# P transposed by VectorE's 32x32 blocks and a way through DRAM, in all attention steps of a gated cross-attention block

## The chip, the cores and the metric

One core of a Trainium2 chip. The metric is the device time of one execution in microseconds (us); the profile gives one execution's span from the first to the last instruction.

## The reference

Eight batches of 128 tokens with 512 features attend to 128 context tokens each, with 32 heads of width 128; a gated feed-forward with low-rank experts follows.

```python
def xattn(hidden, kv, mask, bias, ln_w, w_q, w_k, w_v, w_out):
    x = rmsnorm(hidden, ln_w)
    h_q, h_k, h_v = heads(x @ w_q.T), heads(kv @ w_k.T), heads(kv @ w_v.T)
    score = einsum('bqhd,bkhd->bhqk', h_q, h_k) + position_bias[None]
    score = where(m, score, -inf)
    score = where(m, softmax(score, axis=-1), 0.0)
    attn = einsum('bhqk,bkhd->bqhd', score, h_v).reshape(b, lq, H * DH)
    return hidden + attn @ w_out.T

x = x + tanh(g_xattn[0]) * xattn(layernorm(x), ctx, mask, ...)
x = x + tanh(g_ffn[0]) * ffn(layernorm(x), ...)   # base + LoRA experts, top 2 of 8
```

## The kernel before

The host only lays arrays out. Four stages follow each other. First the V product for all heads, spilled to DRAM (`v_spill`). Then the attention stage: 16 pairs of heads with four steps each, 64 steps (`s = 4 * p + j`), one step for one head and four of the eight batches (`HT`). Then the output product over 56 units, and the feed-forward. The large products are written as seven half-size products (M1 to M7) in place of eight, and each fp32 operand is split into a high and a low fp32r part, so that a product is three passes (`three_passes`, line 328).

The order of the work is written out by hand, one program for each engine, joined by semaphores. In the attention stage TensorE's step `s` does the scores of step `s + 1`, two or one products of the next pair's Q and K (`SLOT_PRODUCTS`), the four transposes of P (`transposes`), more products, and the attention of step `s`. In the last pair the output units 0 to 7 take the place of the products.

Each product needs its weights split. ScalarE makes the high part (`wq_hi`, line 797), VectorE the low part (`lo`, line 1014) and the sums of weights (`wq_sum`, lines 1133 to 1147), both directly after the product whose place in a ring of four units (`WRING`) is free; ScalarE copies and VectorE adds the products out of PSUM (`product_done`).

The softmax of a step: VectorE adds scores and masked bias (`scores`, line 1180, from bank 1 to the SBUF tile `pr`) and takes the negative maximum (1182); ScalarE takes the exponential of four 128x128 blocks with their sums (`softmax_exp`, 860); VectorE inverts the sums (1188), multiplies them with `allowed` (1190) and multiplies P (1193, `probabilities`, the last work of VectorE's step); TensorE transposes P into bank 2; ScalarE copies it to `pt_sb` (916); TensorE multiplies it with V (`attention`, 1531); ScalarE copies the result (`copy_attention`, 898). GpSimd prepares the masked bias (`mask_step`) and forms sums of attention results (`t_sum`, at the steps of `T_SUMS`).

One queue, SP's, issues every DMA, in program order: stores of attention results and their sums (`store_at`, `store_sums`), loads of V (`load_v`), of weights (`load_wq`) and of bias, pieces of the output weight (`load_piece`, `store_piece`), and late in the stage the first loads of the output stage (`EARLY_LOADS`, whose splits are at `EARLY_SPLITS`). A wait there holds up all that is queued behind it.

Of the kernel before, what the change touches and what calls it, by code (L numbers as in the profile page):

```python
# [61 lines left out]
T_SUMS = ((1, 0, 3), (1, 1, 5), (2, 1, 6), (2, 0, 7), (3, 1, 7), (4, 0, 8), (3, 0, 9), (4, 1, 10))  # L62
# [23 lines left out]
def flamingo_block(nc, x, ctx_t, mask, gates, bias, ln_w, w_qk, w_v, w_o, w_base, w_lora, w_up, b_base, out):  # L86
    v_dram = nc.dram_tensor("v_spill", (PAIRS, 2, 2, P, HALF, P), F32, kind="Internal").ap()
    t_dram = nc.dram_tensor("t_spill", (NP, DUOS, P, 2, W), F32, kind="Internal").ap()
    s_dram = nc.dram_tensor("s_spill", (NP, DUOS, P, 2, 2 * P), F32, kind="Internal").ap()
    stack = ExitStack()  # L90
    with stack:
# [46 lines left out]
        with second:  # L138
# [7 lines left out]
            pt_sb = sb("pt_sb", [P, W], on=second)  # L146
            pr = sb("pr", [P, 2, W], on=second)
# [61 lines left out]
        ps_s, ps_t, ps_at = bank[1], bank[2], bank[3]  # L209
# [30 lines left out]
        t_ps, pt_ok, a_ps, at_ok = sem("t_ps"), sem("pt_ok"), sem("a_ps"), sem("at_ok")  # L240
# [66 lines left out]
        def cols(k):  # L307
            return slice(P * k, P * k + P)

# [55 lines left out]
        def _(sp):  # L365
# [23 lines left out]
            def store_v(g, m):  # L389
                r, n = QUARTER[m]  # L390
                for t in range(HALF):
# [6 lines left out]
                    sp.dma_start(dst, stage[:, t, :, :]).then_inc(v_stored[t], 16)  # L398

# [122 lines left out]
            for p in range(PAIRS):  # L522
                if p + 2 < PAIRS:
                    sp.wait_ge(wq_lo_ok, NP * (p + 1))
                    load_wq(p + 2)
                for j in range(4):
                    s = 4 * p + j
                    store_at(s)
                    if s + VRING < STEPS:
                        sp.wait_ge(a_ps, s + 1)  # L530
                        load_v(s + VRING)
                    store_sums(s)
                    if s % 2 == 0 and s + 2 < STEPS:
                        store_piece(s // 2)
                    elif s % 2 and s + 1 < STEPS:
                        load_piece((s + 1) // 2)
                    if j == 2 and p + 2 < PAIRS:
                        sp.wait_ge(bm_ok, 4 * p + 4)
                        load_bias(p + 2)
                    for n in EARLY_LOADS.get((p, j), ()):  # L540
                        load_o(n)

            store_piece(STEPS // 2 - 1)
            for n in range(FIRST_LOAD, UNITS):
                load_o(n)
                if n < FIRST_LOAD + 3:
# [30 lines left out]
        def _(pool):  # L577
# [129 lines left out]
            for s in range(STEPS, STEPS + 3):  # L707
                t_sums(s)
# [18 lines left out]
        def _(act):  # L727
# [129 lines left out]
            def softmax_exp(s):  # L857
                act.wait_ge(nmax_ok, s + 1)
                for k in range(HALF):
                    last = act.activation(pr[:, s % 2, cols(k)], pr[:, s % 2, cols(k)], ACT.Exp, bias=nmax[:, k:k + 1],  # L860
                                          accum_out=sums[:, k:k + 1])
                last.then_inc(exp_ok, 1)

# [60 lines left out]
            copy_attention(STEPS - 1)  # L924
# [53 lines left out]
            for n in range(FIRST_SPLIT, 50):  # L978
                o_hi(n)
# [32 lines left out]
        def _(ve):  # L1012
# [162 lines left out]
            def scores(s):  # L1175
                ve.wait_ge(s_ps, s + 1)
                ve.wait_ge(bm_ok, s + 1)
                if s >= 2:
                    ve.wait_ge(t_ps, s - 1)
                ve.tensor_tensor(pr[:, s % 2, :], ps_s[:, :], bm[:, :, :].rearrange("p b n -> p (b n)"), ALU.add).then_inc(scored, 1)  # L1180
                ve.wait_ge(scored, s + 1)
                ve.tensor_reduce(nmax[:, :], pr[:, s % 2, :].rearrange("p (b k) -> p b k", b=HALF), AX.X, ALU.max,  # L1182
                                 negate=True).then_inc(nmax_ok, 1)

            def probabilities(s):
                n = HT[s % 4][1]
                ve.wait_ge(exp_ok, s + 1)
                ve.reciprocal(rinv[:, :], sums[:, :]).then_inc(inv_ok, 1)
# [557 lines left out]
```

## Time and profile before

| | |
|---|---|
| median of 3 runs | 820.06 us (819.56 to 820.52) |
| profiled execution | span 817.2 us; its time outside the span is not shown |
| busy | TensorE 99%, VectorE 78%, ScalarE 61%, GpSimd 36% |
| granted TensorE clock | 1.000 |
| DMA | 168.52 MB, 63.0% of 16 engines' span |

Busy shares are means over all stages; the attention stage is read by windows and by the instructions in order of time. The chain is the work that ended last, followed back from the end.

### The profile page before, as it was taken

To read this page: it belongs to the slowest core of one execution; us is meant where nothing else is said; L and a number is where in the kernel's file an instruction comes from. 1 tells how busy PE (TensorE), PEld (TensorE's weight loads), DVE (VectorE), ACT (ScalarE), POOL (GpSimd) and SP (SyncE) were. 2 spreads that over 40 slices of the span, in tenths; PEclk is the share of its full clock that TensorE was granted. 3 is DMA by queue.
4 is the path that set the end of the run, shared out by engine and by line. 5 is a ranking of instruction groups with operands and counts; after the bars stand their busy time and mean duration, and the time that the engine had idled before them with its cause. 6 is when DMAs were issued, how large, how long until landed. Compare 5 with 4: busy or idle time off the path is not lost.

```text
span 817.2 us, 13043 instructions
## 1 busy us (share of the span) xinstructions
PE 810.3 (99%) x4286; PEld 689.3 (84%) x4286; DVE 638.7 (78%) x997; ACT 497.1 (61%) x1164; POOL 294.5 (36%) x309
## 2 busy tenths in 40 slices
PE   9999999999999999999999999999999999999998
PEld 7787887888888888888888888888888788888886
DVE  6976476557887898688888888977887976789875
ACT  4646655447666666766666666667677677666311
POOL 1113230002456365455555563564733600003230
PEclk9999999999999999999999999999999999999999
DMA  9565455688545665565575466655598999997011
GB/s 324 157 194 169 118 165 168 218 247 257 168 146 190 189 199 161 193 212 149 180 220 173 147 192 187 189 172 193 173 308 308 367 387 386 328 325 263 20 46 59
DMA packets 132594, 168.52 MB, mean 206 GB/s; under 512 B 9392, under 2 KB 84016, under 8 KB 132272
## 3 DMA queue, kind: packets, MB, share of 16 engines
q1 hardware_dynamic: 132528, 167.70, 63.0%
q8 instruction: 35, 0.57, 0.3%
q14 instruction: 31, 0.25, 0.1%
HBM read 111.04 MB, written 62.91 MB: 213 GB/s over the span
## 4 chain that ended last, share of the span: by engine, by line
PE 90%; DVE 7%; issue 1%; ACT 1%; POOL 1%; DMA 1%; DVEq 0%; SPq 0%; POOLq 0%
PE bank L328 71%; PE bank L1514 7%; PE bank L1531 7%; PE bank L1522 3%; DVE t_hl L1014 1%; DVE s_hl L1014 1%; DVE stats L1018 1%; DVE wv L1014 1%; DMA raw_v<-in_w_v 1%; PE bank L1620 0%; PE bank L1457 0%; DVE stage L1075 0%; DVE acc L1250 0%; POOL xs L598 0%; DVE cb L1014 0%
## 5 line engine op out<-in xcount | busy, mean ns | idle before, releaser
L328 PE MATMUL bank<-cb,wq 128*128 128x512 f32 x672 | 177.2, 399 | 0.0
L328 PE MATMUL bank<-xb,wq 128*128 128x512 f32 x672 | 177.2, 399 | 0.0
L328 PE MATMUL bank<-t_hl,s_hl 128*128 128x512 f32 x672 | 158.0, 393 | 0.1
L328 PE MATMUL bank<-wv,cb 128*128 128x512 f32 x672 | 154.7, 391 | 1.5 <-DVE wv L1014 1.1
L328 PEld LDWEIGHTS bank<-wv,cb 128*128 128x128 f32 x672 | 125.6, 188 | 29.6 <-DVE wv L1014 3.0
L328 PEld LDWEIGHTS bank<-t_hl,s_hl 128*128 128x128 f32 x672 | 124.6, 188 | 26.2 <-DVE s_hl L1014 0.6
L654 POOL TENSOR_TENSOR bm<-bias_sb,mneg 128x512 f32<-128x512 f32 x64 | 74.6, 1166 | 197.4 <-DVE pr L1180 161.5
L328 PEld LDWEIGHTS bank<-cb,wq 128*128 128x128 f32 x672 | 121.9, 189 | 22.8
L328 PEld LDWEIGHTS bank<-xb,wq 128*128 128x128 f32 x672 | 121.8, 189 | 22.7
L860 ACT ACTIVATE pr<-pr,nmax 128x128 f32<-128x128 f32 x256 | 99.3, 394 | 7.2 <-DVE nmax L1182 7.2
L1014 DVE TENSOR_TENSOR t_hl<-t_raw,t_hl 128x1024 fp32r<-128x1024 f32 x56 | 72.1, 1287 | 21.0 <-ACT t_hl L871 20.8
L871 ACT ACTIVATE t_hl<-t_raw 128x1024 fp32r<-128x1024 f32 x56 | 59.3, 1059 | 41.8 <-PE bank L328 31.9
L1014 DVE TENSOR_TENSOR wq<-sq,wq 128x512 fp32r<-128x512 f32 x64 | 67.2, 1060 | 10.0 <-ACT wq L797 10.0
L1014 DVE TENSOR_TENSOR wq<-raw,wq 128x512 fp32r<-128x512 f32 x48 | 38.9, 812 | 42.9 <-ACT wq L797 42.7
L1531 PEld LDWEIGHTS bank<-pt_sb,v_sb 128*128 128x128 f32 x512 | 66.9, 191 | 5.0
L1514 PE MATMUL bank<-k_sb,q_sb 128*128 128x128 f32 x512 | 67.6, 275 | 0.0
L1531 PE MATMUL bank<-pt_sb,v_sb 128*128 128x128 f32 x512 | 67.3, 274 | 0.0
L1514 PEld LDWEIGHTS bank<-k_sb,q_sb 128*128 128x128 f32 x512 | 62.5, 192 | 0.2
L797 ACT ACTIVATE wq<-sq 128x512 fp32r<-128x512 f32 x64 | 40.1, 628 | 26.0 <-PE bank L328 26.0
L1180 DVE TENSOR_TENSOR pr<-bank,bm 128x512 f32<-128x512 f32 x64 | 43.9, 686 | 9.2 <-PE bank L1514 9.2
L860 ACT ACTIVATION_READ_ACCUMULATOR pr<-pr,nmax 128x1 f32 x256 | 49.5, 193 | 0.0
L1193 DVE TENSOR_TENSOR pr<-pr,rinv 128x512 f32<-128x512 f32 x64 | 46.1, 720 | 2.2
(158 smaller groups left out, 1169.9 us busy)
## 6 DMA issues: line engine op xcount, KB each, us to landing
t_raw<-t_spill SPq DMA_DIRECT2D x56, 512.0 KB, 5.5
v_spill<-stage SPq DMA_DIRECT2D x64, 256.0 KB, 3.1
raw<-in_w_qk SPq DMA_DIRECT2D x32, 512.0 KB, 5.8
v_sb<-v_spill SPq DMA_DIRECT2D x64, 256.0 KB, 3.1
s_raw<-s_spill SPq DMA_DIRECT2D x56, 256.0 KB, 5.6
t_spill<-x_at SPq DMA_DIRECT2D x48, 256.0 KB, 3.3
s_piece<-in_w_o SPq DMA_DIRECT2D x64, 128.0 KB, 3.5
s_spill<-s_piece SPq DMA_DIRECT2D x32, 256.0 KB, 3.6
```

The costliest lines, as they stand in the source:

```text
L328: mm = pe.matmul(dst, a, b, start=first and n == 0, stop=last and n == total - 1, skip_group_check=True)
L654: pool.tensor_tensor(bm[:, :, :], head_bias, mneg[:, HALF * n:HALF * n + HALF, :], ALU.add).then_inc(bm_ok, 1)
L797: act.activation(wq[:, u % WRING, 0, :, :], wq_source(p, m), ACT.Copy).then_inc(wq_hi_ok, 1)
L860: last = act.activation(pr[:, s % 2, cols(k)], pr[:, s % 2, cols(k)], ACT.Exp, bias=nmax[:, k:k + 1], accum_out=sums[:, k:k + 1])
L871: act.activation(t_hl[n % ORING][:, 0, :, :], t_raw[n % ORING][:, :, :], ACT.Copy).then_inc(o_hi_ok, 1)
L1014: return ve.tensor_tensor(dst, src, hi.bitcast(F32), ALU.subtract)
L1018: ve.bn_stats(stats[:, t, :], source(t)).then_inc(bn_sem, 1)
L1180: ve.tensor_tensor(pr[:, s % 2, :], ps_s[:, :], bm[:, :, :].rearrange("p b n -> p (b n)"), ALU.add).then_inc(scored, 1)
L1193: ve.tensor_tensor(own, own, rinv[:, :].unsqueeze(2).to_broadcast([P, HALF, P]), ALU.mult).then_inc(pr_ok, 1)
L1514: last = pe.matmul(ps_s[:, cols(k)], q_sb[:, j, cols(k)], k_sb[:, j, cols(k)], start=True, stop=True)
L1522: last = pe.transpose(ps_t[:, cols(k)], pr[:, s % 2, cols(k)], ident[:, :])
L1531: last = pe.matmul(ps_at[:, cols(k)], v_sb[:, s % VRING, k, :], pt_sb[:, cols(k)], start=True, stop=True)
```

## The change

TensorE's transposes and ScalarE's copy of P are gone. The scores of a step are written to one of two PSUM banks (1 and 2) and stay there: VectorE adds the bias in place, ScalarE takes the exponential in place, and ScalarE, not VectorE, multiplies P by the inverse sums (`scale_rows`). VectorE then turns P by 32x32 blocks from PSUM into the SBUF tile `turned` (`turn`, the first work of its step). SP stores the four groups of 32 partitions with four DMAs to DRAM (`p_spill`), so that the blocks come to their places, and loads the whole with one DMA into one of two tiles `pt`. Attention reads its four batches from it in runs of 32 columns, and stands one step later; the copy, the store of its result, the load of V and GpSimd's sums move with it. The attention of the last step stands behind output unit 9.

```diff
-T_SUMS = ((1, 0, 3), (1, 1, 5), (2, 1, 6), (2, 0, 7), (3, 1, 7), (4, 0, 8), (3, 0, 9), (4, 1, 10))
+T_SUMS = ((1, 0, 4), (1, 1, 6), (2, 1, 7), (2, 0, 8), (3, 1, 8), (4, 0, 9), (3, 0, 10), (4, 1, 11))
+LATE_SUMS = 4
+LAST_ATTENTION = 9
+QUADS = 4
+QUAD = P // QUADS
+TURN_EVERY = 1
...
+    p_dram = nc.dram_tensor("p_spill", (2, P, QUADS, P), F32, kind="Internal").ap()
...
-        ps_s, ps_t, ps_at = bank[1], bank[2], bank[3]
+        pr, ps_at = [bank[1], bank[2]], bank[3]
...
+        def pt_batch(s, k):
+            return pt[:, s % 2, :].rearrange("p (i k q) -> p k i q", i=QUADS, k=HALF)[:, k, :, :]
...
+            def store_turned(s):
+                sp.wait_ge(turned_ok, turns(s) + 1)
+                for i in range(QUADS):
+                    sp.dma_start(p_dram[turns(s) % 2, :, i, :].rearrange("(j c) n -> c j n", j=QUADS),
+                                 turned[QUAD * i:QUAD * i + QUAD, :].rearrange("c (j n) -> c j n", j=QUADS)).then_inc(turned_stored, 16)
+            def load_pt(s):
+                sp.wait_ge(turned_stored, 16 * QUADS * (turns(s) + 1))
+                if s >= 2:
+                    sp.wait_ge(a_ps, s - 1)
+                sp.dma_start(pt[:, s % 2, :], p_dram[turns(s) % 2, :, :, :].rearrange("p i n -> p (i n)")).then_inc(pt_in[s % 2], 16)
...
             for p in range(PAIRS):
                 for j in range(4):
                     s = 4 * p + j
+                    if by_quads(s):
+                        store_turned(s)
+                    if j == 0 and p + 2 < PAIRS:
+                        sp.wait_ge(wq_lo_ok, NP * (p + 1))
+                        load_wq(p + 2)
+                    if s % 2 and s + 1 < STEPS:
                         store_piece(s // 2)
                     if j == 2 and p + 2 < PAIRS:
                         sp.wait_ge(bm_ok, 4 * p + 4)
                         load_bias(p + 2)
+                    if by_quads(s):
+                        load_pt(s)
+                    store_sums(s)
+                    if s:
+                        store_at(s - 1)
+                        if s - 1 + VRING < STEPS:
+                            sp.wait_ge(a_ps, s)
+                            load_v(s - 1 + VRING)
+                    if s % 2 and s + 1 < STEPS:
+                        load_piece((s + 1) // 2)
...
+            def scale_rows(s):
+                act.wait_ge(inv_ok, 2 * s + 2)
+                into = pr[s % 2]
+                for k in range(HALF):
+                    last = act.activation(into[:, cols(k)], pr[s % 2][:, cols(k)], ACT.Copy, scale=rinv[:, k:k + 1])
+                last.then_inc(pr_ok, 1)
...
-                    copy_attention(s - 1)
+                    scale_rows(s)
+                    copy_attention(s - 2)
                     for n in range(done, done + before):
                         product_done(n)
-                    act.wait_ge(t_ps, s + 1)
-                    if s:
-                        act.wait_ge(a_ps, s)
-                    act.activation(pt_sb[:, :], ps_t[:, :], ACT.Copy).then_inc(pt_ok, 1)
                     if s + 1 < STEPS:
                         softmax_exp(s + 1)
...
-                ve.wait_ge(inv_ok, 2 * s + 2)
-                own = pr[:, s % 2, :].rearrange("p (b k) -> p b k", b=HALF)
-                ve.tensor_tensor(own, own, rinv[:, :].unsqueeze(2).to_broadcast([P, HALF, P]), ALU.mult).then_inc(pr_ok, 1)
+            def turn(s):
+                ve.wait_ge(pr_ok, s + 1)
+                if turns(s):
+                    ve.wait_ge(turned_stored, 16 * QUADS * turns(s))
+                ve.transpose(turned[:, :].rearrange("p (j k n) -> p j k n", j=QUADS, k=HALF),
+                             pr[s % 2][:, :].rearrange("p (k j n) -> p j k n", k=HALF, j=QUADS)).then_inc(turned_ok, 1)
...
+                    if by_quads(s):
+                        turn(s)
                     if s + 1 < STEPS:
                         scores(s + 1)
...
             def attention(s):
-                pe.wait_ge(pt_ok, s + 1)
+                pe.wait_ge(pt_in[s % 2], 16 * (s // 2 + 1))
...
-                        for n in range(done, done + before):
-                            product(n)
-                    else:
-                        output(2 * j)
-                    transposes(s)
-                    if p + 1 < PAIRS:
-                        for n in range(done + before, done + before + after):
+                        for n in range(done, done + before + after):
                             product(n)
                         done += before + after
                     else:
+                        output(2 * j)
                         output(2 * j + 1)
-                    attention(s)
+                    if s:
+                        attention(s - 1)
```

## Rows read from the trace of the kernel before

**Rows 1.** The page: busy time of each engine, and the chain by engine.
```profile
PE 810.3 (99%) x4286; PEld 689.3 (84%) x4286; DVE 638.7 (78%) x997; ACT 497.1 (61%) x1164; POOL 294.5 (36%) x309
...
PE 90%; DVE 7%; issue 1%; ACT 1%; POOL 1%; DMA 1%; DVEq 0%; SPq 0%; POOLq 0%
```

**Rows 2.** Window: busy us of PE, PEld, DVE, ACT, POOL; clock, DMA share, GB/s.
```profile
300.00:600.00 300.00, 300.00 (x1746) 260.91 (x1745) 248.06 (x393) 199.05 (x583) 158.91 (x169) 1.00 0.59 185
```

**Rows 3.** The chain in order of time: start us, us, what, 380 to 420 us.
```profile
386.48 0.44 PE bank L1522 x4
...
389.68 0.89 PE bank L1531 x8
...
400.55 0.44 PE bank L1522 x4
```

**Rows 4.** Groups of VectorE: busy us, mean ns of one, idle before.
```profile
L1014 DVE TENSOR_TENSOR t_hl<-t_raw,t_hl 128x1024 fp32r<-128x1024 f32 x56 | 72.1, 1287 | 21.0 <-ACT t_hl L871 20.8
L1014 DVE TENSOR_TENSOR wq<-sq,wq 128x512 fp32r<-128x512 f32 x64 | 67.2, 1060 | 10.0 <-ACT wq L797 10.0
...
L1180 DVE TENSOR_TENSOR pr<-bank,bm 128x512 f32<-128x512 f32 x64 | 43.9, 686 | 9.2 <-PE bank L1514 9.2
...
L1143 DVE TENSOR_TENSOR sq<-raw 128x512 f32<-128x512 f32 x16 | 18.4, 1150 | 0.0
...
L1133 DVE TENSOR_TENSOR sq<-raw 128x512 f32<-128x512 f32 x16 | 10.9, 684 | 0.2 <-DMA raw<-in_w_qk 0.2
...
L1258 DVE TENSOR_SCALAR xn<-acc,mv,scales 128x512 f32<-128x512 f32 x8 | 4.2, 542 | 0.6 <-POOL scales L714 0.6
```

**Rows 5.** Groups of ScalarE.
```profile
L916 ACT ACTIVATE pt_sb<-bank 128x512 f32<-128x512 f32 x64 | 37.9, 592 | 15.4 <-PE bank L1522 15.4
L873 ACT ACTIVATE s_hl<-s_raw 128x512 fp32r<-128x512 f32 x56 | 34.5, 616 | 0.0
...
L782 ACT ACTIVATE tok<-bank,lnw 128x512 f32<-128x512 f32 x8 | 4.8, 688 | 1.3 <-PE bank L1457 1.3
...
L946 ACT ACTIVATE h_sum<-bank 128x136 f32<-128x136 f32 x8 | 1.8, 281 | 6.1 <-PE bank L1622 6.1
```

**Rows 6.** ScalarE in order of time, in two stretches: start us, us, instruction.
```profile
393.85 0.40 ACT L860 ACTIVATE pr<-pr,nmax 128x128 f32<-128x128 f32 x1
...
395.39 0.58 ACT L846 ACTIVATE tmp<-bank 128x512 f32<-128x512 f32 x1
395.87 0.62 ACT L797 ACTIVATE wq<-raw 128x512 fp32r<-128x512 f32 x1
...
797.52 0.46 ACT L946 ACTIVATE h_sum<-bank 128x136 f32<-128x136 f32 x2 [1.20 <-PE bank L1622]
```

**Rows 7.** VectorE in order of time, 396 to 399 us.
```profile
396.52 0.69 DVE L1014 TENSOR_TENSOR wq<-raw,wq 128x512 fp32r<-128x512 f32 x1 [1.28 <-ACT wq L797]
...
397.73 0.17 DVE L1188 RECIPROCAL rinv<-sums 128x4 f32<-128x4 f32 x1
397.94 0.16 DVE L1190 TENSOR_TENSOR rinv<-rinv,allowed 128x4 f32<-128x4 f32 x1
398.13 0.69 DVE L1193 TENSOR_TENSOR pr<-pr,rinv 128x512 f32<-128x512 f32 x1
398.74 0.68 DVE L1180 TENSOR_TENSOR pr<-bank,bm 128x512 f32<-128x512 f32 x1
```

**Rows 8.** Who waited for whom: us in total, times, longest us.
```profile
DVE wq L1014 <- ACT wq L797: 52.7, 52, 2.5
```

**Rows 9.** DMA issues: KB each, median us from issue to landing.
```profile
v_spill<-stage SPq DMA_DIRECT2D x64, 256.0 KB, 3.1
raw<-in_w_qk SPq DMA_DIRECT2D x32, 512.0 KB, 5.8
v_sb<-v_spill SPq DMA_DIRECT2D x64, 256.0 KB, 3.1
```

**Rows 10.** SP's issues in order of time.
```profile
405.68 0.43 SPq L410 DMA_DIRECT2D v_sb<-v_spill  x1
```

More of the change, by code:

```diff
@@ L145, in flamingo_block @@
             bm = sb("bm", [P, HALF, P], on=second)
-            pt_sb = sb("pt_sb", [P, W], on=second)
-            pr = sb("pr", [P, 2, W], on=second)
+            turned = sb("turned", [P, W], on=second)
+            pt = sb("pt", [P, 2, W], on=second)
             x_at = sb("x_at", [P, 2, W], on=second)
@@ L308, in cols, with by_quads, turns @@
             return slice(P * k, P * k + P)
+        def by_quads(s):
+            return s % TURN_EVERY == TURN_EVERY - 1
+        def turns(s):
+            return s // TURN_EVERY
+        def pt_batch(s, k):
+            return pt[:, s % 2, :].rearrange("p (i k q) -> p k i q", i=QUADS, k=HALF)[:, k, :, :]
         def v_evac(g, m, t):
@@ L545, in _ @@
                 load_o(n)
-                if n < FIRST_LOAD + 3:
+                if n < FIRST_LOAD + LATE_SUMS:
+                    if n == FIRST_LOAD + LATE_SUMS - 2:
+                        store_at(STEPS - 1)
                     store_sums(STEPS + n - FIRST_LOAD)
@@ L706, in _ @@
             s_sums(STEPS // 2 - 1)
-            for s in range(STEPS, STEPS + 3):
+            for s in range(STEPS, STEPS + LATE_SUMS):
                 t_sums(s)
@@ L859, in softmax_exp @@
                 for k in range(HALF):
-                    last = act.activation(pr[:, s % 2, cols(k)], pr[:, s % 2, cols(k)], ACT.Exp, bias=nmax[:, k:k + 1],
+                    last = act.activation(pr[s % 2][:, cols(k)], pr[s % 2][:, cols(k)], ACT.Exp, bias=nmax[:, k:k + 1],
                                           accum_out=sums[:, k:k + 1])
                 last.then_inc(exp_ok, 1)
+            def scale_rows(s):
[4 more added lines that the diff above has]
+                last.then_inc(pr_ok, 1)
             def o_hi(n):
@@ L1177, in scores @@
                 ve.wait_ge(bm_ok, s + 1)
-                if s >= 2:
-                    ve.wait_ge(t_ps, s - 1)
-                ve.tensor_tensor(pr[:, s % 2, :], ps_s[:, :], bm[:, :, :].rearrange("p b n -> p (b n)"), ALU.add).then_inc(scored, 1)
+                own = pr[s % 2][:, :]
+                ve.tensor_tensor(own, own, bm[:, :, :].rearrange("p b n -> p (b n)"), ALU.add).then_inc(scored, 1)
                 ve.wait_ge(scored, s + 1)
-                ve.tensor_reduce(nmax[:, :], pr[:, s % 2, :].rearrange("p (b k) -> p b k", b=HALF), AX.X, ALU.max,
+                ve.tensor_reduce(nmax[:, :], own.rearrange("p (b k) -> p b k", b=HALF), AX.X, ALU.max,
                                  negate=True).then_inc(nmax_ok, 1)
@@ L1510, in scores @@
                     pe.wait_ge(ed_ok, 6 * p + 2 * j + 2)
-                if s:
-                    pe.wait_ge(scored, s)
+                if s >= 2:
+                    pe.wait_ge(turned_ok, s - 1)
                 for k in range(HALF):
-                    last = pe.matmul(ps_s[:, cols(k)], q_sb[:, j, cols(k)], k_sb[:, j, cols(k)], start=True, stop=True)
+                    last = pe.matmul(pr[s % 2][:, cols(k)], q_sb[:, j, cols(k)], k_sb[:, j, cols(k)], start=True, stop=True)
                 last.then_inc(s_ps, 1)
-            def transposes(s):
-                if s:
-                    pe.wait_ge(pt_ok, s)
-                pe.wait_ge(pr_ok, s + 1)
-                for k in range(HALF):
-                    last = pe.transpose(ps_t[:, cols(k)], pr[:, s % 2, cols(k)], ident[:, :])
-                last.then_inc(t_ps, 1)
             def attention(s):
-                pe.wait_ge(pt_ok, s + 1)
+                pe.wait_ge(pt_in[s % 2], 16 * (s // 2 + 1))
                 pe.wait_ge(v_in[s % VRING], 16 * (s // VRING) + 16)
@@ L1530, in attention @@
                 for k in range(HALF):
-                    last = pe.matmul(ps_at[:, cols(k)], v_sb[:, s % VRING, k, :], pt_sb[:, cols(k)], start=True, stop=True)
+                    last = pe.matmul(ps_at[:, cols(k)].rearrange("p (i q) -> p i q", i=QUADS), v_sb[:, s % VRING, k, :],
+                                     pt_batch(s, k), start=True, stop=True)
                 last.then_inc(a_ps, 1)
@@ L1644, in _ @@
                 output(n)
+                if n == LAST_ATTENTION:
+                    attention(STEPS - 1)
             out_transposes(0)
```

24 lines of the change are left out of this document (9 added, 15 removed).

## The prediction

> **What bounds the kernel now.** The page first. TensorE's matmuls cover 99% of the span and carry 90% of the chain that ended last [rows 1]: whatever another engine does is free as long as TensorE never waits for it. Then one stretch inside the attention stage, 300 to 600 us [rows 2]. TensorE is busy for the whole 300 us at a granted clock of 1.00 (the level of 2.4 GHz), VectorE for 248.06 and ScalarE for 199.05. Third the chain in order of time [rows 3]: four transposes of P take 0.44 us of it, eight attention matmuls 0.89. The transposes of every second step start 14.07 us apart (386.48 and 400.55), so a step is 7.03 us on average, a pair of heads (four steps, one round of `SLOT_PRODUCTS`) 28.14. In a mean step VectorE works 248.06/300 x 7.03 = 5.82 us and idles 1.22; ScalarE works 4.67. These 1.22 us of VectorE are all the room there is before it sets the pace.
>
> The second thing to read is why VectorE idles at all. Of its waits, 52.7 us in 52 cases are for ScalarE's high part of a weight unit [rows 8]; one is seen at 396.52, 0.03 us behind ScalarE's instruction of 395.87 [rows 6, 7], which had stood behind four exponentials and a copy. So part of that idle time is ScalarE's order and stays when the pace changes.
>
> **TensorE's side.** Removed: `transposes`, 64 x 0.44 = 28.2 us, all on the chain [rows 3]. Scores and attention keep their number of matmuls. P is now read in four runs of 32 columns; no row shows such a read. Below, it costs nothing; above, I bound it by a quarter more of the 0.89 us, 0.2 per step, within what TensorE gains. I take nothing: all operands are fp32 in rows as before. If TensorE remained the bound, the span would be 817.2 - 28.2 = 789.0.
>
> **ScalarE's side.** Removed: the copy of P out of PSUM, 0.592 us [rows 5], in a row of copies 0.48. Added: `scale_rows`, four 128x128 activations with a scale read per partition. The nearest row is a 128x136 copy from PSUM, 0.280; a per-partition scale lengthens a 128x512 copy from 0.592 to 0.688, so 0.10 more; one is 0.37 [rows 5]. Two of the 128x136 copies take 0.46 together, so they overlap by 0.10 [rows 6], and four scalings take 3 x 0.27 + 0.37 = 1.18. Bounds: 0.28 + 3 x 0.18 = 0.82 if the scale costs nothing, 4 x 0.40 = 1.60 if each takes an exponential's full record [rows 6]. The exponentials now read PSUM; copies do so in 0.592 where they take 0.616 from SBUF [rows 5], so four go from 4 x 0.385 = 1.54 (393.85 to 395.39 [rows 6]) to 1.44. ScalarE ends near 5.2 us a step and is not the bound by its sum.
>
> The Trainium skill (ScalarE: Activation LUTs, Rules for kernel authors) advises to leave multiplications to VectorE, which speaks against moving this one. Its prices (What ACT_TABLE_LOAD costs: 186 ns plus 0.833 per element, 93 for a pointer operand, 93 of overlap) would make an estimate of 1.27 for the four instead of the 1.18 of the rows, and the sum below 5 us larger. The rows decide.
>
> **VectorE's side.** Removed: the multiplication of P, 0.69, with 0.61 until the next one starts (398.13 to 398.74 [rows 7]). Added: the turn of 128x512 from PSUM, which no row shows. Below, 0.542, the quickest 128x512 instruction; above, 1.287, the instruction over twice the columns [rows 4]. I take 0.69, that of the PSUM operations of this size (L1180), because it reads PSUM at this width; occupancy 0.61. The score addition writes PSUM instead of SBUF; I leave it and the maximum at 0.69. In work VectorE neither gains nor loses.
>
> The Trainium skill (VectorE: DVE Perf Modes, The three transpose paths) gives 311 ns for 128x128 in bf16; four of these, an estimate, would be 1.24 and the sum 60 x 0.55 = 33 us larger; no row here shows a transpose on VectorE.
>
> What counts is the new wait. `probabilities(s)` is the last thing in VectorE's step and `turn(s)` the first of the next, with nothing between. Before, the multiplication followed the inverse by 0.03. Now VectorE hands the inverse over (0.04), stands still for the four scalings (1.18), takes over (0.04) and turns. It loses 1.23 us in every step, queued behind the wait are score addition, maximum, all weight splits and sums, and TensorE waits for those. Occupied time is 5.82 + 1.23 = 7.05 in the mean, already more than 7.03, before any other wait.
>
> **A pair laid out.** From the inverse on: head 0.04 + 1.18 + 0.04 + 0.61 + 0.72 (addition) + 0.60 (maximum) = 3.19 until VectorE is free, and the exponentials start at 3.32. Tail (reciprocal and small product): 0.40, from 397.73 to 398.10 [rows 7] and a little. Weight splits take 1.06 from sums in the mean [rows 4], from raw weights 0.69 undisturbed (396.52 [rows 7]); additions occupy 0.60; the four weight sums, one a step, take 0.684 (the first) to 1.150 (the third) in the mean [rows 4]. The steps of a pair, by `j`:
> Step 0: 3.19 + sum 1.07 + splits 0.90 and 0.80 + addition 0.60 + 0.40 = 6.96. Step 3: 3.19 + two additions 1.20 + split 0.87 + sum 1.10 + 0.40 = 6.76. In both, the splits needed are ready on ScalarE.
> Step 1 hangs on ScalarE: 3.32 + 1.44 (exponentials) + 0.48 (copy of M6) + 0.62 (high part) + 0.03 + split 0.70 + sum 0.62 + 0.40 = 7.61. Step 2 likewise: 3.32 + 1.44 + 0.62 + 0.03 + 0.70 + 0.85 + 0.40 = 7.36.
> Together 28.69. These layouts hold 22.2 us of VectorE's work (four heads without the wait 7.7, four tails 1.6, and 3.4, 2.9, 3.4, 3.2 in the steps, with what runs hidden behind ScalarE in steps 1 and 2), where the rows have 248.06/300 x 28.14 = 23.27; the 1.07 missing are splits and sums that last longer than I set them. Half lies in steps 0 and 3, and a little more behind the waits of 1 and 2: I add 0.65. A pair is 29.34, 7.33 a step, 1.20 more than before.
>
> **DMA and SP.** Per step four stores of 64 KB and a load of 256 KB come on SP's queue, 33.6 MB in all. The landing rows are 3.1 us for the 256 KB store in 512-byte rows and for the V load [rows 9]; issuing takes 0.43 [rows 10]. From the inverse of step s: attention s-2 is copied at 1.73, behind the scalings; SP issues its store, the V load and in odd steps two pieces (to 2.6 or 3.7); four stores (the last begins at 3.9 or 4.9); landed at 7.0 or 8.0; load landed at 10.1 or 11.1. The weight loads, piece store and bias load that are queued behind the four stores fill that wait. `attention(s)` stands at the end of TensorE's next step, takes 0.89 and must be through at 2 x 7.33 - 0.5 = 14.1, since scores and the first product of the step behind it are wanted early; 11.1 + 0.89 = 12.0, so at least 2 us are left, which hide the way. The next turn waits for the stores until 8.0 and comes at 7.33 + 1.26 = 8.6. GpSimd's sums move by one step with their sources and cost nothing, hidden in its 53% of use [rows 2]. With 0.5 MB more per step the DMA share goes from 0.59 [rows 2] to some 0.8.
>
> **The sum.** Fifteen pairs x 1.20 = +18.0. In the last pair the splits of the output stage stand between inverse and turn on VectorE and hide the scalings; there TensorE stays the bound: 4 x 0.44 = -1.8. Span 817.2 + 18.0 - 1.8 = 833.4. The median of the three runs, 820.06, is 2.9 above the span; with that, 836.
>
> **Rivals and chances.** 0.2% is about what a measurement here can tell from no change.
> The forecast, slower: 0.56, own range 824 to 848.
> The wait fits into VectorE's idle time, faster: 0.20 (0.04 of it within 0.2%). For it: 1.22 idle against 1.23 lost. Against it: the idle time behind ScalarE's order. It turns on the four scalings: without them a pair is 29.34 - 4 x 1.18 = 24.62, so below 3.52/4 = 0.88 us from inverse to turn the time falls. With 0.82 and no slowed splits a pair is 28.69 - 4 x 0.36 = 27.25; fifteen times -0.89 less 1.8 and plus 2.9 is 805; halfway to break-even about 812.
> TensorE stays the bound all through: 789.0 + 2.9 = 792, chance 0.08. For it stands only the page's 99%.
> The turn costs as two passes, 1.287: 0.60 more per step, 60 x 0.60 = 36, 872; chance 0.10.
> The way through DRAM binds: 0.06. It decides from landings of (14.1 - 0.89 - 4.9)/2 = 4.2 us on, and the 512 KB weight loads do take 5.8 [rows 9]; at 4.5 the odd steps are 0.6 late, 30 x 0.6 = 18, 854. Beside it, the Trainium skill (DMA: Bandwidth & Descriptors, Rules for kernel authors) calls transfers below 64 KB mostly overhead and asks to join them; these stores are of just that size, and no row shows one.
> Faster 0.16 + 0.08 = 0.24; within 0.2% 0.04 and 0.03 of the forecast's lower end, 0.07; slower 0.53 + 0.10 + 0.06 = 0.69. The range 806 to 858 leaves out the 792 and the 872, together 0.18.
>
> **What would show it.** Right: VectorE idle before the turn by 1.2 us, 60 times, released by ScalarE's scalings; turns of 0.69; score additions 7.3 us apart; TensorE idle some 0.7 us a step before products, released by VectorE's splits; P landed 2 us or more before attention. Wrong: TensorE without gaps (then the waits overlap what I added up), turns far from 0.69, or attention matmuls waiting for a DMA.

## The result, and the profile after

| | before | after |
|---|---|---|
| median | 819.9 us (819.56 to 820.52) | 876.45 us (873.57 to 878.15) |
| ratio | | 1.0683 [1.0668, 1.0699] |
| profiled span | 817.2 us | 875.3 us |
| granted TensorE clock, mean | 1.000 | 0.969 |

Slower, as forecast, but by 56.6 us where 16 were forecast, and outside the range of 806 to 858. The page of the changed kernel, busy time and the chain by engine, answers to [rows 1]:

```profile
PE 809.0 (92%) x4030; PEld 680.5 (78%) x4030; DVE 634.2 (72%) x997; ACT 519.1 (59%) x1356; POOL 285.7 (33%) x309
...
PE 36%; DVE 20%; DMA 16%; SPq 11%; issue 10%; ACT 7%; POOL 1%; DVEq 0%; ACTq 0%; POOLq 0%
```

TensorE held 90% of the chain and holds 36% now. The first thing to ask is where in the span the 58.1 us arose. VectorE's negative maximum is taken once a step and marks its place; here are those of steps 1, 57 and 63, before (line 1182) and after (line 1229):

```profile
188.36 0.69 DVE L1182 TENSOR_REDUCE nmax<-pr 128x4 f32<-128x512 f32 x1
...
582.28 0.69 DVE L1182 TENSOR_REDUCE nmax<-pr 128x4 f32<-128x512 f32 x1
...
627.93 0.69 DVE L1182 TENSOR_REDUCE nmax<-pr 128x4 f32<-128x512 f32 x1
```

```profile
190.44 0.69 DVE L1229 TENSOR_REDUCE nmax<-bank 128x4 f32<-128x512 f32 x1
...
606.92 0.69 DVE L1229 TENSOR_REDUCE nmax<-bank 128x4 f32<-128x512 f32 x1
...
675.07 0.69 DVE L1229 TENSOR_REDUCE nmax<-bank 128x4 f32<-128x512 f32 x1
```

The differences are the first two lines of this table; the same subtraction gives a line for most of the experiments below (us, from one profiled execution each):

| kernel | to step 1 | steps 1 to 57 (one step) | 57 to 63 | 63 to the end | span |
|---|---|---|---|---|---|
| before | 188.4 | 393.9 (7.03) | 45.7 | 189.3 | 817.2 |
| after | 190.4 | 416.5 (7.44) | 68.2 | 200.2 | 875.3 |
| scores first | 188.4 | 410.6 (7.33) | 57.0 | 210.9 | 867.0 |
| VectorE multiplies | 189.1 | 404.5 (7.22) | 66.3 | 200.0 | 859.9 |
| scores first, no landing wait | 188.6 | 389.8 (6.96) | 51.6 | 196.6 | 826.5 |
| turn first, no landing wait | 189.9 | 411.1 (7.34) | 59.4 | 193.2 | 853.6 |
| last eight steps by TensorE | 190.2 | 414.2 (7.40) | 46.1 | 194.6 | 845.1 |
| scores first and last eight | 188.0 | 406.0 (7.25) | 49.3 | 195.4 | 838.7 |
| all steps by TensorE | 187.7 | 394.4 (7.04) | 45.5 | 194.4 | 822.0 |
| output loads behind the stores | 190.1 | 420.6 (7.51) | 55.2 | 196.4 | 862.3 |
| every other step by TensorE | 187.9 | 383.4 (6.85) | 46.5 | 195.3 | 813.1 |

So the loss lies in three places: 22.6 us in the 56 usual steps, 22.5 in the six late ones and 10.9 behind them; the 2.1 at the start are about the handover and the turn of step 0, which stand ahead of the first mark.

Two things bear on how the table is read. Where VectorE takes the scores first, the maximum stands ahead of the turn, so the marks lie earlier in a step; late losses of such a line are compared by the sum of its last two columns (before 235.0, after 268.4). And single executions scatter: the usual steps of the change stand all but unaltered in the lines with the last eight steps by TensorE (414.2) and with the loads behind the stores (420.6), those of the scores first also in the line with both (406.0 for 410.6).

**The usual steps.** Windows of the changed kernel (busy us of PE, PEld, DVE, ACT, POOL; clock, DMA share, GB/s), the first answering to [rows 2]:

```profile
300.00:600.00 300.00, 278.38 (x1521) 238.66 (x1521) 237.28 (x379) 203.71 (x683) 149.51 (x165) 0.98 0.81 245
600.00:640.00 40.00, 30.95 (x154) 25.59 (x152) 24.05 (x36) 21.20 (x68) 15.78 (x17) 0.89 0.81 256
640.00:660.00 20.00, 16.51 (x79) 14.55 (x80) 11.43 (x19) 11.41 (x34) 6.58 (x8) 0.80 0.70 210
660.00:680.00 20.00, 11.43 (x54) 9.27 (x53) 10.74 (x16) 10.16 (x29) 2.44 (x2) 0.88 0.76 236
```

Who waited for whom, 300 to 600 us (us in total, times, longest):

```profile
DVE turned L1246 <- ACT bank L910: 43.7, 37, 1.2
DVE wq L1062 <- ACT wq L838: 10.8, 13, 1.4
DVE turned L1246 <- DMA p_spill<-turned: 6.5, 4, 1.9
...
PE bank L1579 <- DMA pt<-p_spill: 21.6, 13, 2.7
```

VectorE's 237.28 us of work and its three waits make 298.3 of 300: it has no time left, and no wait of its own is for TensorE. All of TensorE's idle time (300 - 278.38 = 21.6) stands ahead of attention, for P; no wait for VectorE's splits is in its list. One handover (VectorE gives the inverse to ScalarE and stands until the four scalings are done) in VectorE's order of time, then ScalarE's part of it, to be held against [rows 6, 7]:

```profile
399.84 0.16 DVE L1239 TENSOR_TENSOR rinv<-rinv,allowed 128x4 f32<-128x4 f32 x1
401.18 0.72 DVE L1246 STREAM_TRANSPOSE turned<-bank 128x512 f32<-128x512 f32 x1 [1.18 <-ACT bank L910]
401.82 0.67 DVE L1227 TENSOR_TENSOR bank<-bank,bm 128x512 f32<-128x512 f32 x1
402.53 0.69 DVE L1229 TENSOR_REDUCE nmax<-bank 128x4 f32<-128x512 f32 x1
```

```profile
400.04 1.11 ACT L910 ACTIVATE bank<-bank,rinv 128x128 f32<-128x128 f32 x4 [1.18 <-DVE rinv L1239]
401.05 0.62 ACT L947 ACTIVATE y_at<-bank 128x512 f32<-128x512 f32 x1
```

**The late steps.** DMA issues of 600 to 680 us (KB each, median us from issue to landing), then the pieces of the chain that belong to P's stores:

```profile
t_raw<-t_spill SPq DMA_DIRECT2D x11, 512.0 KB, 6.3
s_raw<-s_spill SPq DMA_DIRECT2D x11, 256.0 KB, 6.5
...
p_spill<-turned SPq DMA_DIRECT2D x31, 64.0 KB, 4.8
```

```profile
619.53 5.13 DMA p_spill<-turned
...
632.69 7.26 DMA p_spill<-turned
...
643.77 5.26 DMA p_spill<-turned
...
654.04 5.69 DMA p_spill<-turned
...
667.37 6.26 DMA p_spill<-turned
```

These five make 29.6 us of the chain in 54 (619.53 to 673.63). Over the whole span the stores land in a median of 2.9 us and P's load in 3.0:

```profile
p_spill<-turned SPq DMA_DIRECT2D x256, 64.0 KB, 2.9
pt<-p_spill SPq DMA_DIRECT2D x64, 256.0 KB, 3.0
```

In the late steps, with the output stage's loads issued ahead of them on the same queue, the stores land in 4.8 (and 5 to 7 on the chain). In every step SP itself stands still for the landing (the completion) of the four stores before it issues P's load:

```profile
SPq L432 <- DMA p_spill<-turned: 136.9, 64, 6.8
```

That is 2.1 us a step in which SP issues nothing of what is queued behind.

### The profile page after: what moved, and what is told of

It is laid out like the page before. It is cut to its first block, busy times and chain, and to the rows that moved or that the text cites. A ratio compares the mean times of both kernels' runs of the same rounds, so it can differ in the third digit from the quotient of the medians.

```text
span 875.3 us, 13104 instructions
## 1 busy us (share of the span) xinstructions
PE 809.0 (92%) x4030; PEld 680.5 (78%) x4030; DVE 634.2 (72%) x997; ACT 519.1 (59%) x1356; POOL 285.7 (33%) x309
## 4 chain that ended last, share of the span: by engine, by line
PE 36%; DVE 20%; DMA 16%; SPq 11%; issue 10%; ACT 7%; POOL 1%; DVEq 0%; ACTq 0%; POOLq 0%
PE bank L348 31%; DMA p_spill<-turned 11%; SPq L424 4%; DMA pt<-p_spill 3%; DVE wq L1062 3%; ACT bank L910 3%; DVE bank L1227 2%; SPq L479 2%; PE bank L1579 2%; SPq L490 2%; DVE t_hl L1062 2%; PE bank L1570 1%; ACT bank L901 1%; DVE nmax L1229 1%; DVE s_hl L1062 1%
## 5 line engine op out<-in xcount | busy, mean ns | idle before, releaser
L348 PEld LDWEIGHTS bank<-xb,wq 128*128 128x128 f32 x672 | 125.3, 191 | 29.6 <-issue 4.8
L910 ACT ACTIVATE bank<-bank,rinv 128x128 f32<-128x128 f32 x256 | 71.3, 342 | 104.5 <-DVE rinv L1239 104.5
L1579 PE MATMUL bank<-pt,v_sb 128*128 128x128 f32 x512 | 77.4, 299 | 54.6 <-DMA pt<-p_spill 54.5
L901 ACT ACTIVATE bank<-bank,nmax 128x128 f32<-128x128 f32 x256 | 88.0, 353 | 62.3 <-DVE nmax L1229 61.5
L1579 PEld LDWEIGHTS bank<-pt,v_sb 128*128 128x128 f32 x512 | 71.1, 207 | 69.0 <-DMA pt<-p_spill 66.1
L1246 DVE STREAM_TRANSPOSE turned<-bank 128x512 f32<-128x512 f32 x64 | 45.9, 717 | 98.4 <-ACT bank L910 56.7
L920 ACT ACTIVATE t_hl<-t_raw 128x1024 fp32r<-128x1024 f32 x56 | 59.4, 1061 | 44.3 <-PE bank L348 25.0
L1062 DVE TENSOR_TENSOR wq<-sq,wq 128x512 fp32r<-128x512 f32 x64 | 79.0, 1253 | 4.3 <-ACT wq L838 4.2
L1570 PE MATMUL bank<-k_sb,q_sb 128*128 128x128 f32 x512 | 73.4, 291 | 0.0
L1570 PEld LDWEIGHTS bank<-k_sb,q_sb 128*128 128x128 f32 x512 | 68.5, 208 | 0.2
L901 ACT ACTIVATION_READ_ACCUMULATOR bank<-bank,nmax 128x1 f32 x256 | 55.8, 218 | 0.0
L1229 DVE TENSOR_REDUCE nmax<-bank 128x4 f32<-128x512 f32 x64 | 44.2, 691 | 2.2
```

Of the source, the lines that this page charges most:

```text
L348: mm = pe.matmul(dst, a, b, start=first and n == 0, stop=last and n == total - 1, skip_group_check=True)
L901: last = act.activation(pr[s % 2][:, cols(k)], pr[s % 2][:, cols(k)], ACT.Exp, bias=nmax[:, k:k + 1], accum_out=sums[:, k:k + 1])
L910: last = act.activation(into[:, cols(k)], pr[s % 2][:, cols(k)], ACT.Copy, scale=rinv[:, k:k + 1])
L920: act.activation(t_hl[n % ORING][:, 0, :, :], t_raw[n % ORING][:, :, :], ACT.Copy).then_inc(o_hi_ok, 1)
L1062: return ve.tensor_tensor(dst, src, hi.bitcast(F32), ALU.subtract)
L1229: ve.tensor_reduce(nmax[:, :], own.rearrange("p (b k) -> p b k", b=HALF), AX.X, ALU.max, negate=True).then_inc(nmax_ok, 1)
```

## The experiments

**VectorE takes the next scores first.** So the scalings on ScalarE are covered by work and the handover costs no wait.

```diff
-                    if by_quads(s):
-                        turn(s)
                     if s + 1 < STEPS:
                         scores(s + 1)
+                    if by_quads(s):
+                        turn(s)
```

> Only VectorE's order changes: the score addition and the maximum of the next step stand before the turn, so that they fill the 1.18 us in which ScalarE scales P. Theory A (the wait for the scalings sets the pace of the first 57 steps, 7.44 us against 7.03 before; the last seven are held by the way through DRAM): those steps fall to 6.6 to 6.9, the idle time before the turn to below 0.2, the last seven stay slow: 830 to 846. Theory B (the way through DRAM sets the pace in all steps): steps stay at 7.4, 870 to 878. Theory C (ScalarE's added work sets it): likewise 870 to 878.

Measured: 870.97 us (869.05 to 872.88), ratio 1.0624 [1.0567, 1.0681]. A miss: the wait for the scalings has left the list, most steps run at TensorE's pace (5.88 and 7.24 us in turn), yet some last 9 to 12. One of them in the chain:

```profile
427.44 4.80 DMA p_spill<-turned
...
432.25 3.52 DMA pt<-p_spill
...
435.82 2.07 PE bank L1579 x8
```

The stores of P landed in 4.80 us beside 1 MB of weights, SP stood in line for them, and only then issued the load. Behind the first limit stands a second that costs as much. From step 57 on nothing is gained (57.0 + 210.9 = 267.9 us against 268.4).

**The multiplication stays on VectorE** (in the PSUM bank), ScalarE scales nothing.

```diff
-                    scale_rows(s)
...
+                ve.tensor_tensor(own, own, rinv[:, :].unsqueeze(2).to_broadcast([P, HALF, P]), ALU.mult).then_inc(pr_ok, 1)
```

> P is multiplied by VectorE again, in its PSUM bank, and turned right behind it; ScalarE scales nothing. Theory A: the wait of 1.18 us is replaced by an instruction that occupies 0.61, a step is 0.5 shorter (6.9), the last seven stay slow: 845 to 855. Theory B: steps stay at 7.4, 870 to 878. Theory C: steps of 7.0 or less as well, since ScalarE has 1.1 us less to do.

Measured: 864.42 us (861.81 to 867.03), ratio 1.0544 [1.0468, 1.0621]. A miss: it lies between the expected ranges, and the steps go from 7.44 to 7.22 where 6.9 was expected. The wait is gone for 0.70 us of work, and the late steps stay at 66.3: the handover cost something, and not the most.

**The last eight steps transposed by TensorE again**, all else as in the change.

```diff
-            return s % TURN_EVERY == TURN_EVERY - 1
+            return s < LATE0
...
+                        act.activation(pt[:, s % 2, :], pr[s % 2][:, :], ACT.Copy).then_inc(pt_ok, 1)
...
+                    last = pe.transpose(pr[s % 2][:, cols(k)], turned[:, cols(k)], ident[:, :])
```

> Steps 56 to 63 are transposed by TensorE (ScalarE scales P into SBUF, TensorE transposes it into the bank that it came from, ScalarE copies it out), the other 56 steps are as changed. Theory A: the first 56 steps stay at 7.4 us, the last seven fall from some 11 to 7, no more waits of TensorE for P from DRAM above 3 us, granted clock back at 1.00 from 600 us on: 840 to 850. Rival D (the last steps are slow because attention stands one step later and the last one behind output unit 9): they stay slow, 870 or more.

Measured: 847.06 us (846.85 to 847.28), ratio 1.0333 [1.0303, 1.0363]. As expected: 29 us come back from eight steps; steps 57 to 63 take 46.1 us, those of before. So the late loss comes with the turn and its way through DRAM. It isn't the handover, for without that the late steps still took 66.3 (the run above); and attention a step later, which stays here, isn't it either.

**Both of these.** The scores first, and the last eight steps by TensorE.

> Scores first in VectorE's order and the last eight steps by TensorE, both together. With scores first the usual steps took 5.9 and 7.2 us in turn, TensorE's own pace, but about every eighth took 9 to 12, TensorE waiting for P from DRAM. Theory A2 (two loops of nearly the same length: the wait for the scalings, and the way through DRAM with SP's order around it): the gains of the two parts add up, some 5 and 29: 840 to 845. If the late steps had been what held the scores-first version as a whole, the first 56 steps would now take 6.6: below 815.

Measured: 843.35 us (840.6 to 846.1), ratio 1.0277 [1.0234, 1.032]. As expected; with the late steps out of the way, VectorE's order is worth some 3.7 us, less than the 5.5 between the two runs of this kernel.

**All steps by TensorE** (`LATE0 = 0`), two score banks, ScalarE's scaling and attention a step later kept.

> All 64 steps transposed by TensorE; the two banks, the scaling by ScalarE and the later attention stay. Theory A: without turn and DRAM nothing waits for the scalings in VectorE's order, TensorE is the bound again at 7.0 to 7.1 us a step: 815 to 828. Theory C (ScalarE, now with scaling and copy): steps of 7.4 or more, 843 or more.

Measured: 823.95 us (823.93 to 824.97), ratio 1.0058 [1.0035, 1.0081]. As expected. The steps are those of before (7.04); 5.1 us are lost behind step 63. The rest of the change costs 4 us, and the other 52.5 hang on the turn and its way.

**Weights behind P's load** (scores first). If the 1 MB of weights ahead of the load delays P, it should gain.

```diff
-                    if j == 0 and p + 2 < PAIRS:
-                        sp.wait_ge(wq_lo_ok, NP * (p + 1))
-                        load_wq(p + 2)
...
                     if by_quads(s):
                         load_pt(s)
+                    if j == 0 and p + 2 < PAIRS:
+                        sp.wait_ge(wq_lo_ok, NP * (p + 1))
+                        load_wq(p + 2)
```

> Scores first, and SP issues the two weight loads of 512 KB behind the load of P instead of between its stores and its load. Theory A2a (the load of P stands behind that megabyte): the steps with j = 0 that took 9 to 12 us fall to 7 to 8, the first 57 steps from 7.33 to 6.7 to 6.9: 835 to 850. Rival A2b (any four stores and a load in a row take too long, whatever is between): 864 to 874.

Measured: 899.21 us (898.94 to 899.48), ratio 1.0958 [1.0936, 1.098]. A miss on the wrong side. SP's waits with the scores first and here, and a wait of VectorE here:

```profile
SPq L432 <- DMA p_spill<-turned: 137.9, 64, 5.2
...
SPq L432 <- DMA p_spill<-turned: 172.6, 64, 6.4
...
DVE sq L1181 <- DMA raw<-in_w_qk: 31.4, 13, 3.6
```

SP's wait for the landing grows by 34.7 us, since the weights no longer fill a part of it and now stand ahead of the next step's stores. But the weights also come later: VectorE stands 31.4 us for them before the first of its sums, a wait of 0.5 us in 300 to 600 with the scores first and of 20.0 here. How the 28 us divide between the two is not shown, so the run does not tell what the weights ahead of P's load cost by themselves.

**P's stores and load issued by GpSimd** (scores first), so that SP waits for nothing of P.

```diff
-                    if by_quads(s):
-                        store_turned(s)
...
+                pool.dma_start(pt[:, s % 2, :], p_dram[turns(s) % 2, :, :, :].rearrange("p i n -> p (i n)")).then_inc(pt_in[s % 2], 16)
```

> Scores first, and GpSimd issues the stores and the load of P, so they neither wait behind SP's other issues nor hold them up; bytes and rows are the same. If the order on SP's queue is what makes P late: steps near 6.6, and the last seven shorter as well: 800 to 835. If it is the amount of DMA work: at 868 or above, with landings as long as now. If GpSimd is slow to issue 320 DMAs: masked bias and sums late, above 871.

Measured: 919.44 us (918.59 to 920.3), ratio 1.1204 [1.1181, 1.1227]. The third case, a GpSimd slowed by the issues. The wait only changed its queue:

```profile
POOL pt L732 <- DMA p_spill<-turned: 136.7, 62, 6.3
...
PE bank L1577 <- DMA pt<-p_spill: 82.7, 37, 7.5
```

GpSimd now stands still for 2.2 us a step, and its own five issues a step count as work: in 300 to 600 us it is busy for 229.2 and waits 61.9 for landings, so nearly no time is left, and TensorE waits 82.7 us for P (52.4 with the scores first). The run frees SP's line but fills GpSimd, and so does not settle what SP's line alone is worth.

**No wait for the landing**, with the scores first:

```diff
-                sp.wait_ge(turned_stored, 16 * QUADS * (turns(s) + 1))
...
-                sp.dma_start(pt[:, s % 2, :], p_dram[turns(s) % 2, :, :, :].rearrange("p i n -> p (i n)")).then_inc(pt_in[s % 2], 16)
+                sp.dma_start(pt[:, s % 2, :], w_v[turns(s) % 2, :, 0:W]).then_inc(pt_in[s % 2], 16)
```

> Scores first, and the load into the P tile reads as many bytes in the same rows from the V weights in DRAM, so that SP doesn't wait in line for the four stores to land; the stores are made as before and VectorE waits for them. It leaves out P: attention multiplies V by weights. DMA count and bytes are unchanged. If SP's wait for the landing, in line ahead of its other issues, makes P late (A2): the first 57 steps fall from 7.33 to near TensorE's 6.6, the late steps gain too: 800 to 830. If the amount of DMA work or the row size does it: 855 or above.

Measured: 827.34 us (826.27 to 828.4), ratio 1.0092 [1.0071, 1.0113]. In the expected range, though a step takes 6.96 us and not near 6.6. The kernel leaves P out of attention (its tile is filled from the weights of V), and the same bytes move, faster; 300 to 600 us:

```profile
300.00:600.00 300.00, 289.11 (x1619) 249.19 (x1618) 243.67 (x402) 219.71 (x732) 150.43 (x172) 1.00 0.88 266
```

The DMA share rises from 0.81 to 0.88 and the time falls by 43.6 us against the scores first alone: the volume is no limit, the wait for the landing is. Whether it costs by holding SP's line or by lengthening P's own way is not separated: without it the tile of P is also filled sooner, 7.2 us behind the turn in the median of steps 14 to 55, against 8.9. What is left above 6.6 lies mostly in the steps whose load stands behind the 1 MB of weights; TensorE still waits 9.5 us for that tile in 300 to 600.

**The same with the turn first**, as in the change. This fills the fourth corner.

> The changed kernel with VectorE's order as it is in the change (the turn first, then the next scores), and with SP's wait for the landing of P's stores gone: the tile of P is loaded from the weights of V, at the same size and place in SP's order, so the attention of P is left out, as in the experiment with the scores first. If the handover to ScalarE and the landing are two limits of which the slower one counts, then the handover alone sets the pace of the usual steps here: 7.1 to 7.3 us a step against 6.96 with the scores first, and with the later steps as they were with the scores first the time is 838 to 852. If the handover cost something only because it made the stores late, it costs nothing any more: 6.9 to 7.0 us a step, and 824 to 832. If the two add up, the time is that of the change less the 43.6 us that the landing was worth with the scores first: 833.

Measured: 856.6 us (855.42 to 859.42), ratio 1.0453 [1.0432, 1.0475]. The waits of 300 to 600 us:

```profile
DVE turned L1245 <- ACT bank L909: 46.1, 39, 1.2
DVE wq L1061 <- ACT wq L837: 10.3, 12, 1.7
DVE turned L1245 <- DMA p_spill<-turned: 4.7, 3, 1.8
```

7.34 us a step where 7.1 to 7.3 were expected, and from step 57 on slower than supposed (252.6 us to the end, not 248.2), so the time is 5 us above the first theory's range; the two others, at 824 to 833, are ruled out. The handover alone costs 411.1 - 393.9 = 17.2 us over steps 1 to 57, the landing alone 410.6 - 393.9 = 16.7 (12.1 in the other execution of these steps), both 22.6 (20.3 and 26.7 in the two others), neither -4.1. Against the kernel with neither, each alone costs some 21 us and both 26.7: far from the sum of 42, and some 5 above the larger. They are two limits side by side rather than two terms of a sum.

**The output stage's loads behind the stores**, the change otherwise whole.

```diff
                     if by_quads(s):
                         store_turned(s)
+                    for n in EARLY_LOADS.get(divmod(s - 1, 4), ()):
+                        load_o(n)
...
-                    for n in EARLY_LOADS.get((p, j), ()):
-                        load_o(n)
```

> The changed kernel whole; only the loads of the output stage that are issued in its last two pairs of heads (512 and 256 KB, one or two pairs a step) go behind the next step's four stores of P instead of ahead of them. In the changed kernel the stores of P take 4.8 us to land in the median of 600 to 680 us against 2.9 over the whole span, and five steps there have stores of 5.1 to 7.3 us on the chain. If the large loads ahead of them in the queue are what delays them, they land in 3 to 3.5 us here, the six steps from the maximum of step 57 to that of step 63 take 54 to 60 us instead of 68.2, and the time is 862 to 870. If it is the volume then under way, whatever the order, the stores still land in 4.5 us or more and the time is 872 to 882. If the loads then delay P's own load instead, that one goes from 2.9 to 5 us or more, and the time is within 5 us of the change's 876 with the wait seen on TensorE for P.

Measured: 862.52 us (860.57 to 864.55), ratio 1.0516 [1.0489, 1.0542]. As expected. DMA issues of 600 to 680 us, and a piece of the chain:

```profile
pt<-p_spill SPq DMA_DIRECT2D x9, 256.0 KB, 4.6
...
p_spill<-turned SPq DMA_DIRECT2D x36, 64.0 KB, 2.5
```

```profile
637.19 7.68 DMA pt<-p_spill
```

The stores land in 2.5 us instead of 4.8, and 13 of the 22.5 late us come back: the loads ahead of them in the queue had delayed them, and not the volume, for more is moved in that time (269 GB/s against 240). A part of that is handed on, since P's load now stands behind the loads (4.6 for 2.9).

**Three of four steps through DRAM** (scores first, every fourth and the last eight by TensorE).

> As the mixed run, but three of four steps up to 55 go through VectorE and DRAM and only those with j = 0 (where the weight loads stand on SP's queue) and the last eight go through TensorE. 42 steps in place of 28 save TensorE 0.44 us: 6 us below the mixed run if TensorE stays the bound, 804 to 811. A2 (each P then has little more than a step for its way again, SP's landing wait in three of four steps): no gain or a loss, 812 to 830.

Measured: 821.35 us (817.61 to 825.37), ratio 1.0027 [1.0007, 1.0048]. No gain is left, as the second case had it: SP waits for the landing in all 42 such steps, 81.3 us, 1.9 each.

**Every other step through DRAM** (scores first; odd steps up to 55, the others by TensorE).

```diff
-            return s % TURN_EVERY == TURN_EVERY - 1
+            return s % 2 == 1 and s < 56
```

> Scores first; odd steps up to 55 go through VectorE and DRAM, even steps and the last eight through TensorE (P scaled into the tile that holds it, transposed into its bank, copied back). 28 steps save TensorE 0.44 us each, 12 us, and the way through DRAM has two steps for each P. Theory A2: TensorE is the bound nearly throughout, 806 to 816. If scaling and copies in ScalarE's order cost more than that, as the 4 us that the all-TensorE run lost: 816 to 826.

Measured: 815.18 us (813.09 to 815.4), ratio 0.9926 [0.9907, 0.9946]: as expected, and 0.7% faster than the kernel before. TensorE has no gaps, and the DMA share is lower:

```profile
300.00:600.00 300.00, 299.92 (x1723) 260.97 (x1722) 237.72 (x382) 232.42 (x762) 158.53 (x177) 1.00 0.75 234
```

## Why the direction was right and the size wrong

**The handover: right.** Four scalings 1.11 us (1.18 forecast), the wait of the turn 1.18 (1.23), the turn 0.717 (0.69). The Trainium skill's 311 ns for a 128x128 bf16 transpose (VectorE: DVE Perf Modes, The three transpose paths) had led to an estimate of 1.24; the trace does not agree with that extrapolation, and the row of the PSUM operation of this size was the better guide. With that the rival of two passes fell. The strided read of P was taken as free, and is: the kernel with every other step through DRAM has both reads side by side, P from DRAM in runs of 32 columns (its line 1602) and in whole rows (line 1605), at 275 and 274 ns a matmul.

```profile
L1605 PE MATMUL bank<-pt,v_sb 128*128 128x128 f32 x288 | 37.9, 274 | 0.0
L1602 PE MATMUL bank<-pt,v_sb 128*128 128x128 f32 x224 | 29.7, 275 | 1.5 <-DMA pt<-p_spill 1.4
```

**The pace of a usual step: right as a mechanism, its last digit by luck.** 7.33 us was worked out for VectorE's loop; the run that has the handover and no landing wait gives 7.34, and in the change VectorE is at work or in its waits for 298.3 of 300 us. So the rivals by which the wait fits into idle time, or TensorE stays the bound, fell. The parts of the layout are not met as closely: in that run, from inverse to inverse, step 0 of a pair takes 8.1 where 6.96 was laid out, and steps 1 to 3 take 7.4, 7.1 and 6.4 in the median for 7.61, 7.36 and 6.76. The two splits of step 0, set at 0.90 and 0.80, take 3.44 together:

```profile
486.68 3.44 DVE L1061 TENSOR_TENSOR wq<-sq,wq 128x512 fp32r<-128x512 f32 x2
```

The 0.65 that the forecast added for longer splits, and a few late steps in the run, bring the two means together. The change as a whole takes 7.44, since the landing adds some 5.4 us over 56 steps (416.5 - 411.1; 3 to 10 by the two other executions of these steps). The DMA share came out at 0.81 for some 0.8.

**"At least 2 us are left, which hide the way": the first step that failed.** Step 28 can be followed in SP's and TensorE's order of time:

```profile
403.12 1.96 SPq L424 DMA_DIRECT2D p_spill<-turned  x4
405.12 0.92 SPq L436 DMA_DIRECT2D raw<-in_w_qk  x2
407.80 0.33 SPq L432 DMA_DIRECT2D pt<-p_spill  x1
```

```profile
412.22 1.16 PE L1579 MATMUL bank<-pt,v_sb 128*128 128x128 f32 x8 [1.10 <-DMA pt<-p_spill]
```

Its inverse was done at 400.00 (399.84 + 0.16). The stores have landed at 7.8 us behind that, where 7.0 to 8.0 was forecast; but the load, behind 1 MB of weights, lands at 12.2 and not at 11.1, 4.4 us from its issue where the median of the span is 3.0. Of the 2 us one is left by the forecast's reckoning, and yet TensorE has stood still for 1.10: it came to attention earlier than the forecast allowed. In 300 to 600 us P comes late to TensorE 13 times, 21.6 us in all. That is a sign which the prediction named for being wrong, and the one that it named for being right, idle time of TensorE released by VectorE's splits, is missing. The forecast took one landing time for every step, and counted SP's stand in its own line as filled by the weight loads, a piece or a bias; these are issues of 0.4 to 0.9 us a step, and SP still stands 2.1 us a step. The rival in which the way binds was given 0.06 and 854 us; its condition, two landings of 4.2 us each, is met where large loads stand ahead in the queue, in such usual steps for the load alone, in the late ones for the stores. With the handover taken away it is the bound by itself (410.6 us, 7.33 a step).

**"There TensorE stays the bound: -1.8": the step that cost most.** For the last pair I looked at VectorE's work alone and left out that in the last two pairs SP issues 768 KB units of the output stage, ahead of P's stores. The six steps from 57 to 63 lose 22.5 us, all of it with the turn and P's way (46.1 us without them, 45.7 before). The order in the queue is 13.0 us of that (68.2 - 55.2), the landing wait by itself 8.8 (68.2 - 59.4). The shares can overlap, and how the rest divides is open. The Trainium skill (DMA: Bandwidth & Descriptors, Rules for kernel authors) asks to join transfers under 64 KB; the prediction quoted it beside its 0.06. The traces agree that a 64 KB store takes nearly as long to land (2.9 us) as a 256 KB load (3.0), but no run here joined the stores.

**"GpSimd's sums move by one step and cost nothing": these, or another part of the rest, cost 4 us.** With every step by TensorE the rest of the change still costs 4 us, behind step 63. Which of its parts (attention a step later, the sums moved, the last store moved) does it was not tried.

**What is left of the sum.** Forecast for the span +16.2: about 17 in the usual steps, next to nothing elsewhere. Measured +58.1: 22.6 + 22.5 + 10.9 + 2.1. So of the 42 us that the forecast missed, some 6 lie in the usual steps and nearly all the rest from step 57 on. Of the 10.9 behind step 63 the rest of the change has 5.1; the other 5.8 go with the late steps (5.6 come back when TensorE does them). The granted clock goes along: from 680 to 760 us it is 0.94 in the change and 1.00 with the last eight steps by TensorE, which for TensorE at work throughout would be 4.8 us, an estimate.

## What to carry to other kernels

A store whose landing the issuing queue waits for holds up that queue's whole line (2.1 us a step here): lay out every queue's line for a full round of steps, and again for the stretch in which the next stage's loads begin, before calling a way through DRAM hidden. Where two limits lie side by side, removing one shows little (5 to 6 of 27 us over the usual steps here); the four corners, with each alone, both and neither, show it. An engine relieved in 28 of 64 steps, with the scores first, gained (0.9926) where relief in all of them lost (1.0683): there the slow way has two steps of time for each P.

## What the hardware showed beyond that

- VectorE turns 128x512 fp32 from PSUM to SBUF in 32x32 blocks in 0.717 us, 0.03 more than an addition of that size (0.69); ScalarE's scaled 128x128 copy inside PSUM has a record of 0.342 us and, four in a row, 0.28 each.
- The granted clock fell with TensorE's gaps: 0.80 to 0.89 in 600 to 680 us after, 1.00 with the last eight steps by TensorE (the last row below). After 8.03 us of idling, eight attention matmuls took 2.08 us, ten microseconds later 1.05: the 1.2 GHz level against 2.4.

```profile
643.49 2.08 PE L1579 MATMUL bank<-pt,v_sb 128*128 128x128 f32 x8 [8.03 <-DMA pt<-p_spill]
...
653.00 1.05 PE L1579 MATMUL bank<-pt,v_sb 128*128 128x128 f32 x8
```

```profile
600.00:680.00 80.00, 58.88 (x286) 49.42 (x285) 46.23 (x70) 42.76 (x131) 24.80 (x27) 0.86 0.77 240
...
600.00:680.00 80.00, 77.27 (x420) 64.78 (x419) 58.00 (x76) 60.61 (x161) 38.60 (x36) 1.00 0.87 293
```

- So TensorE's busy time fell by 1.3 us only (810.3 to 809.0), although 256 transposes of 28.2 us were gone. Matmuls at the lower clock fill most of the difference of 26.9: busy time times the share of the clock that was missing, window by window, comes to some 22 to 25 us, an estimate.
- GpSimd was held for 0.55 us by the issue of a store of P and 0.57 by that of its load; SP's queue for 0.46 and 0.34 (medians, in the change).
